# Leaves of the block factorisation: half of T's rows turned by TensorE during the leaf, and one PSUM area per stage

## Chip, cores and metric

One core of a Trainium2 chip. The metric is the device time of one launch in microseconds (us); the median of three runs of the kernel before is 1134.49 us (1133.51 to 1136.28).

## The reference, cut to what matters

The layer is x + FFN/2, then x + attention, then x + FFN/2 (widths 256 and 1024, ternary weights, 8 sequences of 1024 tokens). The change lies in the attention, which is a recurrence over tokens with a 128 x 128 state:

```python
u = k / (norm(k) + EPS)
Au = A @ u;  denom = 1 + u @ Au
A = A - outer(Au, Au) / denom
z = Au / denom
M = M + outer(v, (k @ q) * z)
o = M @ q
```

The kernel computes it in chunks of 128 tokens: 8 chunks of 8 sequences are 64 "pairs", each with a 128 x 128 Gram matrix, and each such matrix is factorised as T K T' = D, with T lower triangular (unit diagonal) and D diagonal. This is done twice: once named "inv" (for the full inverse T) and once named "ldl" (applied to a right side, whose rows replace it).

## The kernel before

Five parts run one after the other: `feed_forward_keys`, `factorise(..., "inv", ...)` (from 332 us of the profiled execution to about 532), `gram`, `factorise(..., "ldl", ...)` (592 to about 795), and `outputs_feed_forward`. Each part is one block: every engine ends it before the next begins.

`factorise` works on all 64 pairs at once. The matrix is cut into NW = 4 block rows of W = 32 columns, and stage r (0 to 3) of a factorisation has a serial part and a wide part.

- The serial part is the **leaf**, on VectorE. `take(r)` (line 999) transposes the 64 diagonal blocks from PSUM so that one lane (partition) holds half a block's rows; `leaf(r)` (L1007 to L1033) runs 32 elimination steps of four instructions (shuffle a row L1011, reciprocal L1014, product L1026, update L1029), each waiting on semaphore `chain` for the one before. It fills `R`, whose columns W to 2W are the rows of the block's T. Then `turn(r)` (L1035) transposes all 32 rows of T, 32 x 32 elements at a time, into `Tt` (L1039, 1024 elements a partition) and the pivots into `dT` (L1040), and raises `turned`. Of the 32 lanes of each quarter in `Tt`, 16 are read later (one for each pair).
- What follows on the way to the next leaf is `finish_diagonal(r + 1)` on TensorE (L1241): it waits for `turned`, multiplies by `Tt` (L1248, 64 products, each two matmuls and two weight loads in the records, so 128 of each), then VectorE (`over_d`, L1052) and ScalarE (`next_block`, L1097) read the result half and half, and a second set of 64 products (L1255) completes the next diagonal block, which `take(r + 1)` reads.
- The wide part runs on TensorE and ScalarE **while VectorE is in the leaf**. TensorE goes through the fills of stage r in program order (`done` L1168, `done right`, `panel` L1203, `panel right`, then `diagonal(r + 1)` L1228), each 4 PSUM banks in size, and ScalarE copies each to SBUF (`empty`, L1099; for `done` with 16 scaled copies more, L1123) and raises `emptied`. In "inv" TensorE also makes the queries and values (`qv`, L1260; 16 in all, 5, 4, 2 and 5 of them in the four stages) and the dot products (`dots`, L1277).
- The fills rotate over the areas in `works` (L789): one area of 4 banks in "inv", which has three other PSUM tiles, and **two areas** in "ldl". `free` (L871) makes a fill wait until the fill before it in the same area has been emptied, or the diagonal in it has been taken. So in "ldl" TensorE may fill one area while ScalarE empties the other.

Both engines take their queues in order. SyncE stores pivots (`keep_d`) and finished rows (`keep_rows`) behind the same semaphores.

Of the kernel before, what the change touches and what calls it, by code (L numbers as in the profile page):

```python
# [12 lines left out]
P = 128  # L13
# [17 lines left out]
W = 32  # L31
RW = W // 2
NW = P // W
NQ = NP // 4


def wait(eng, sem, value):
# [717 lines left out]
def factorise(nc, name, m, c, a=None):  # L755

    first = a is not None  # L760
    with ExitStack() as ctx:
        def sb(what, shape, dt=F32):
# [2 lines left out]
        def psum(what, shape, dt=F32):  # L765
            return ctx.enter_context(nc.psum_tensor(f"{name}_{what}", shape, dt))
# [5 lines left out]
        R = c.R  # L772
# [13 lines left out]
            ZR = sb("right_side", [P, NQ, P])  # L786
            YR = [m.T[:, NQ * k:NQ * (k + 1)] for k in range(NW)]

        works = [psum(f"work{i}", [P, NQ, P]) for i in range(1 if first else 2)]  # L789
        if first:  # L790
            wqv = sb("wqv", [P, DC, 2, H])
            bq = sb("bq_column", [P, 1])
# [10 lines left out]
        lane_reset = sem("lane_reset")  # L803
        chain = sem("lane_chain")
        turned = sem("turned")
        taken = sem("diagonal_taken")
        filled = sem("filled")
        emptied = sem("emptied")
# [6 lines left out]
        if first:  # L815
            w_in = sem("wqv_in")
            a_in = [sem(f"aT_in{s}") for s in range(2)]
            u_in = sem("uT_in")
            q_made = sem("q_product")
            q_done = sem("q_done")  # L820
            v_made = sem("v_product")
            v_done = sem("v_done")
            uq_done = sem("uq_done")
            dots_done = sem("dots_done")
            dots_kept = sem("dots_kept")
            q_stored = sem("q_stored")
            v_stored = [sem(f"v_stored{s}") for s in range(2)]

        def block_of(r):
            return slice(W * r, W * r + W)  # L830
# [63 lines left out]
        with nc.Block() as block:  # L894
# [95 lines left out]
            @block.vector  # L990
            def _(v):
                links = [0]

                def note(ins):
                    links[0] += 1
                    ins.then_inc(chain, 1)
                    return links[0]

                def take(r):

                    v.wait_ge(diag_done, r + 1)
                    nc.vector.transpose(M[:, :, 0:W].rearrange("l r (h p) -> l r h p", h=2),
                                        area(r, "diagonal")[:, :, 0:W].rearrange("i p (r h) -> i r h p", h=2)).then_inc(taken, 1)
                    v.wait_ge(taken, r + 1)
                    v.wait_ge(lane_reset, r + 1)

                def leaf(r):  # L1007
                    for j in range(W):
                        own = j % 2
                        v.wait_ge(chain, links[0])  # L1010
                        row = note(nc.vector.stream_shuffle(R[:, j, j:W + j + 1], M[:, j // 2, j:W + j + 1],  # L1011
                                                            [16 * own + i % 16 for i in range(W)]))
                        v.wait_ge(chain, row)
                        i = nc.vector.reciprocal(dl[:, j:j + 1], R[:, j, j:j + 1])  # L1014
                        if j == W - 1:
                            note(i)
                            break
                        note(i)

                        r0 = (j + 1) // 2
                        n = RW - r0
                        window = slice(j + 1, W + j + 1)
                        shape = [P, n, W]
                        note(nc.vector.tensor_tensor(prod[:, :n], M[:, r0:, j:j + 1].to_broadcast(shape),  # L1026
                                                     R[:, j:j + 1, window].to_broadcast(shape), ALU.mult))
                        v.wait_ge(chain, links[0])
                        i = nc.vector.scalar_tensor_tensor(out=M[:, r0:, window], in0=prod[:, :n],  # L1029
                                                           scalar=dl[:, j:j + 1], in1=M[:, r0:, window],  # L1030
                                                           op0=ALU.mult, op1=ALU.subtract, reverse1=True)
                        note(i)
                    v.wait_ge(chain, links[0])  # L1033

                def turn(r):  # L1035
                    if r:

                        v.wait_ge(filled, fill_number[r, "done" if first else "done right"] + 1)
                    nc.vector.transpose(Tt[:], R[:, :, W:])  # L1039
                    nc.vector.transpose(dT[r][:], dl[:]).then_inc(turned, 1)  # L1040

                def over_d(r):


                    v.wait_ge(turned, r + 1)
                    for half in range(2):
                        pr = slice(8 * half, 8 * half + 8)
                        if half:
                            v.wait_ge(y_done, 2 * r + 1)
                        else:  # L1050
                            v.wait_ge(next_done, r + 1)
                        nc.vector.scalar_tensor_tensor(  # L1052
                            out=YD[r][:, pr, 0:W], in0=area(r + 1, "diagonal")[:, pr, W:2 * W], scalar=-1.0,
                            in1=dT[r][:, pr].unsqueeze(2).to_broadcast([P, 8, W]),
                            op0=ALU.mult, op1=ALU.mult).then_inc(yd_done, 1)

                def times_q(r, which):

                    v.wait_ge(u_in, 16 * (QV_OF[r][-1] + 1))
                    for n in which:  # L1060
                        v.wait_ge(q_done, n + 1)
                        nc.vector.tensor_tensor(uT[:, slot(n)], uT[:, slot(n)], qT[:, slot(n)], ALU.mult
                                                ).then_inc(uq_done, 1)

                for r in range(NW):
                    take(r)
                    leaf(r)
                    turn(r)
                    if r < NW - 1:
                        if first:  # L1070
                            times_q(r, QV_OF[r][:3])
                        over_d(r)
                        if first:
                            times_q(r, QV_OF[r][3:])
                    elif first:
                        times_q(r, QV_OF[r])

            @block.scalar
            def _(act):
# [3 lines left out]
                def reset(r):  # L1083
                    if r:
                        act.wait_ge(turned, r)
                    copy(M[:, :, W:], c.lane_ident[:]).then_inc(lane_reset, 1)

                def next_block(r):

# [60 lines left out]
                for r in range(NW + 1):  # L1150
                    if 0 < r < NW - 1:
                        act.wait_ge(turned, r)
                        nc.scalar.mul(nd[:], dT[r - 1][:, 0:NQ], -1.0).then_inc(nd_done, 1)
                        act.wait_ge(nd_done, r)
                    for i, (what, n) in enumerate(beside(r)):
                        if what is not None:
                            empty(r, what)
                        if first and r and i == 0:
                            keep_dots(r - 1)
                        if n is not None:  # L1160
                            qv(n)
                    if r < NW - 1:
                        reset(r + 1)
                        next_block(r)

            @block.tensor
            def _(pe):
# [60 lines left out]
                def diagonal(r):  # L1228
# [9 lines left out]
                    if r == 0:  # L1238
                        i.then_inc(diag_done, 1)

                def finish_diagonal(r):  # L1241

                    k = r - 1
                    work = area(r, "diagonal")
                    emptied_of(pe, k, "panel")
                    pe.wait_ge(turned, r)
                    for p, q in tile_order():
                        i = nc.tensor.matmul(work[rows_of(q), p, W:2 * W], Tt[rows_of(q), :, p],  # L1248
# [39 lines left out]
                diagonal(0)  # L1288
                for r in range(NW + 1):
                    if r == NW:  # L1290
                        pe.wait_ge(turned, NW)
                    if first and 0 < r < NW:
                        dots(r - 1)
                    if first and r == 0:
                        pe.wait_ge(w_in, 48)
                    opened = r >= NW - 1
                    for what, n in beside(r):
                        if what is not None:
                            (done if what.startswith("done") else panel)(r, what)
                        elif not opened:  # L1300
                            diagonal(r + 1)
                            opened = True
                        if n is not None:
                            qv(n)
                    if not opened:
                        diagonal(r + 1)
                    if first and r == NW:
                        dots(r - 1)
                    if r < NW - 1:
                        finish_diagonal(r + 1)  # L1310

# [586 lines left out]
```

## Time and profile before

| | us |
|---|---|
| median of 3 runs | 1134.49 |
| the profiled execution's own time | 1137.41 |
| its span | 1135.7 |
| busy: TensorE, VectorE, ScalarE | 937.7, 806.5, 527.1 |
| "inv": start of its first diagonal to its last T transpose's end | 332.0 to 521.7 |
| "ldl": the same | 592.9 to 782.3 |

A timeline row gives start, length, engine, line, operation, the output and inputs, the number of instructions merged in it, and in brackets the idle time of the engine before it and what ended that; "issue" there means that the profile shows nothing that it waited for. Matmul rows merge many overlapping instructions.

### The profile page before, as it was taken

The page shows a single profiled execution, that of the slowest core. Times are in us where ns is not written, and L with a number is a line of the kernel's source. Part 1 is how long each engine was busy: PE and PEld are TensorE (multiplying, and loading weights), DVE is VectorE, ACT ScalarE, POOL GpSimd, SP SyncE. Part 2 cuts the span into 40 slices and gives each one's busy share as a digit, 9 for nine tenths or more (in the row PEclk, how much of TensorE's full clock was granted, in tenths as well). Part 3 has the DMA queues.
Part 4 walks back from the last instruction along what each step waited for, and adds up shares of the span by engine and source line. Part 5 has one row for each costly group of instructions (what it writes and reads, how often), then busy time and mean ns, then how long its engine had stood idle before and what let it go on. Part 6 is the DMA issues. An engine that isn't in the chain of part 4 may idle for free. (4 is left out here: it accounts for less than half of the span.)

```text
span 1135.7 us, 28433 instructions
## 1 busy us (share of the span) xinstructions
PE 937.7 (83%) x11466; PEld 724.9 (64%) x11466; DVE 806.5 (71%) x2564; ACT 527.1 (46%) x1083; POOL 300.6 (26%) x254
## 2 busy tenths in 40 slices
PE   4799999999967788686991445692689999999998
PEld 1477777777845667675980434581567777777766
DVE  6877778787659888794559797885366666666663
ACT  4677878777632142121331212101165655656564
POOL 4345344453210000000000000000475464645440
PEclk9999999999988697798996576796699999999999
DMA  5354554644258252154540000056344242434231
GB/s 150 66 131 107 135 130 121 161 110 130 94 173 206 87 159 74 44 156 126 149 129 1 3 2 5 3 151 136 117 102 103 66 121 75 102 94 99 61 75 56
DMA packets 185518, 113.92 MB, mean 100 GB/s; under 512 B 85808, under 2 KB 178352, under 8 KB 184752
## 3 DMA queue, kind: packets, MB, share of 16 engines
q1 hardware_dynamic: 168496, 95.38, 32.9%
q10 hardware_dynamic: 16896, 16.78, 4.8%
q8 instruction: 88, 1.44, 0.5%
q14 instruction: 38, 0.31, 0.1%
HBM read 49.16 MB, written 37.75 MB: 77 GB/s over the span
## 5 line engine op out<-in xcount | busy, mean ns | idle before, releaser
L1664 DVE TENSOR_TENSOR out_h_rest<-out_ps_h,out_h_high 128x512 f16<-128x512 f32 x128 | 88.4, 690 | 100.1 <-ACT out_ps_h L1726 99.4
L1574 POOL TENSOR_TENSOR T<-T,out_bv_rows 128x512 f32<-128x512 f32 x16 | 20.3, 1271 | 478.3 <-DMA out_bv_rows<-in_bqkv 477.3
L1725 ACT ACTIVATE out_h_high<-out_ps_h,b_columns 128x512 f16<-128x512 f32 x128 | 88.1, 689 | 110.8 <-PE out_ps_h L1807 109.7
L410 DVE TENSOR_TENSOR ffn_h_rest<-ffn_ps_h,ffn_h_high 128x512 f16<-128x512 f32 x128 | 87.0, 684 | 53.8 <-ACT ffn_ps_h L580 53.3
L1819 PE MATMUL out_ps_y<-w_ternary,out_h_high 128*128 128x256 f16 x512 | 118.2, 273 | 0.3 <-DVE out_h_rest L1664 0.3
L1819 PE MATMUL out_ps_y<-w_ternary,out_h_rest 128*128 128x256 f16 x512 | 118.2, 273 | 0.0
L579 ACT ACTIVATE ffn_h_high<-ffn_ps_h,b_columns 128x512 f16<-128x512 f32 x128 | 87.8, 686 | 65.0 <-PE ffn_ps_h L653 64.4
L667 PE MATMUL ffn_ps_y<-w_ternary,ffn_h_rest 128*128 128x256 f16 x512 | 117.8, 273 | 0.0
L667 PE MATMUL ffn_ps_y<-w_ternary,ffn_h_high 128*128 128x256 f16 x512 | 117.8, 273 | 0.0
L653 PE MATMUL ffn_ps_h<-ffn_xT_high,w_ternary 128*128 128x512 f16 x256 | 98.7, 386 | 11.7 <-DVE ffn_h_rest L410 11.7
L653 PE MATMUL ffn_ps_h<-ffn_xT_rest,w_ternary 128*128 128x512 f16 x256 | 98.4, 384 | 0.0
L1807 PE MATMUL out_ps_h<-out_xT_high,w_ternary 128*128 128x512 f16 x256 | 97.0, 379 | 0.0
L1807 PE MATMUL out_ps_h<-out_xT_rest,w_ternary 128*128 128x512 f16 x256 | 97.0, 379 | 0.0
L1726 ACT ACTIVATE out_ps_h<-out_ps_h,b_columns 128x512 f32<-128x512 f32 x128 | 84.0, 657 | 0.0
L580 ACT ACTIVATE ffn_ps_h<-ffn_ps_h,b_columns 128x512 f32<-128x512 f32 x128 | 83.9, 655 | 0.0
L1029 DVE SCALAR_TENSOR_TENSOR ldl_lane_matrix<-ldl_rank_one,ldl_lane_dinv,ldl_lane_matrix 128x480 f32<-128x480 f32 (+15 forms) x124 | 61.3, 494 | 4.4
L1029 DVE SCALAR_TENSOR_TENSOR inv_lane_matrix<-inv_rank_one,inv_lane_dinv,inv_lane_matrix 128x480 f32<-128x480 f32 (+15 forms) x124 | 61.3, 494 | 4.4
L1819 PEld LDWEIGHTS out_ps_y<-w_ternary,out_h_high 128*128 128x128 f16 x512 | 50.1, 98 | 17.5 <-DVE out_h_rest L1664 0.6
L667 PEld LDWEIGHTS ffn_ps_y<-w_ternary,ffn_h_rest 128*128 128x128 f16 x512 | 50.1, 98 | 17.0
L1819 PEld LDWEIGHTS out_ps_y<-w_ternary,out_h_rest 128*128 128x128 f16 x512 | 50.1, 98 | 17.0
L667 PEld LDWEIGHTS ffn_ps_y<-w_ternary,ffn_h_high 128*128 128x128 f16 x512 | 50.1, 98 | 16.9
L1248 PE MATMUL ldl_work<-ldl_panel,ldl_T_turned 32*32 32x32 f32 x384 | 6.1, 239 | 63.8 <-DVE ldl_dinv_turned L1040 63.8
(190 smaller groups left out, 2192.1 us busy)
## 6 DMA issues: line engine op xcount, KB each, us to landing
ffn_x<-in_x SPq DMA_DIRECT2D x16, 512.0 KB, 4.8
x_scratch<-ffn_x_out ACTq DMA_DIRECT2D x16, 512.0 KB, 3.3
aT_scratch<-ffn_aT SPq DMA_DIRECT2D x16, 512.0 KB, 5.4
inv_aT<-aT_scratch SPq DMA_DIRECT2D x16, 512.0 KB, 4.7
T<-x_scratch SPq DMA_DIRECT2D x16, 512.0 KB, 3.8
out_x<-out_x ACTq DMA_DIRECT2D x10, 512.0 KB, 3.3
uT_scratch<-ffn_uT SPq DMA_DIRECT2D x16, 256.0 KB, 5.4
inv_uT<-uT_scratch SPq DMA_DIRECT2D x16, 256.0 KB, 4.3
```

The costliest lines, as they stand in the source:

```text
L410: nc.vector.tensor_tensor(hl[n % 2][:, f], ps_h[f % 3][:], hh[n % 2][:, f], ALU.subtract).then_inc(hl_done, 1)
L579: nc.scalar.activation(hh[n % 2][:, f], ps_h[f % 3][:], ACT.Gelu, bias=c.b1[:, f:f + 1])
L580: nc.scalar.activation(ps_h[f % 3][:], ps_h[f % 3][:], ACT.Gelu, bias=c.b1[:, f:f + 1]).then_inc(g_done, 1)
L653: ins = nc.tensor.matmul(ps_h[f % 3][:], c.w1[:, d, f * P:(f + 1) * P], part[s][:, :, d], start=(k == 0), stop=(k == 2 * DC - 1))
L667: ins = nc.tensor.matmul(ps_y[t % 2][:], part[n % 2][:, f, t * P:(t + 1) * P], c.w2[:, f], start=(f == 0 and part is hh), stop=(f == FC - ...
L1029: i = nc.vector.scalar_tensor_tensor(out=M[:, r0:, window], in0=prod[:, :n], scalar=dl[:, j:j + 1], in1=M[:, r0:, window], op0=ALU.mult, o ...
L1574: nc.gpsimd.tensor_tensor(v0[s], v0[s], bv[:].unsqueeze(1).to_broadcast(group), ALU.add).then_inc(biased, 1)
L1664: nc.vector.tensor_tensor(hl[k % 2][:, f], ps_h[f % 3][:], hh[k % 2][:, f], ALU.subtract).then_inc(hl_done, 1)
L1725: nc.scalar.activation(hh[k % 2][:, f], ps_h[f % 3][:], ACT.Gelu, bias=c.b1[:, f:f + 1])
L1726: nc.scalar.activation(ps_h[f % 3][:], ps_h[f % 3][:], ACT.Gelu, bias=c.b1[:, f:f + 1]).then_inc(g_done, 1)
L1807: ins = nc.tensor.matmul(ps_h[f % 3][:], c.w1[:, d, f * P:(f + 1) * P], part[s][:, :, d], start=(j == 0), stop=(j == 2 * DC - 1))
L1819: ins = nc.tensor.matmul(ps_y[t % 2][:], part[k % 2][:, f, t * P:(t + 1) * P], c.w2[:, f], start=(f == 0 and part is hh), stop=(f == FC - ...
```

## The change

A constant EARLY = 16 is added. TensorE gets `turn_early(r)`: once row 15 of the leaf has been shuffled into `R`, 64 products of 128 x 32 elements of `R` with 16 columns of the unit matrix put the first 16 rows of T, turned, into a new PSUM tile `ps_t` (1 KB a partition, so one bank). It stands after all fills of stage r and after `diagonal(r + 1)`, ahead of `finish_diagonal(r + 1)`. ScalarE gets `early_rows(r)`, one copy of 256 elements a partition from `ps_t` to `Tt`, after all its emptying of stage r. VectorE's transpose at the leaf's end covers the other 16 rows. `finish_diagonal` and the last `done` wait for the copy too. `works` has one area in both factorisations.

```diff
+EARLY = W // 2
...
-        works = [psum(f"work{i}", [P, NQ, P]) for i in range(1 if first else 2)]
+        works = [psum("work", [P, NQ, P])]
+        ps_t = psum("ps_t", [P, EARLY, NQ])
...
+        CHAIN = 4 * W - 2
...
                         v.wait_ge(filled, fill_number[r, "done" if first else "done right"] + 1)
-                    nc.vector.transpose(Tt[:], R[:, :, W:])
+                    nc.vector.transpose(Tt[:, EARLY:], R[:, EARLY:, W:])
                     nc.vector.transpose(dT[r][:], dl[:]).then_inc(turned, 1)
...
+                def early_rows(r):
+                    act.wait_ge(early_made, r + 1)
+                    if r:
+
+                        act.wait_ge(filled, fill_number[r, "done" if first else "done right"] + 1)
+                    copy(Tt[:, :EARLY, 0:NQ], ps_t[:]).then_inc(early_done, 1)
...
+                    if r < NW:
+                        early_rows(r)
                     if r < NW - 1:
                         reset(r + 1)
                         next_block(r)
...
+                def turn_early(r):
+
+                    pe.wait_ge(chain, r * CHAIN + 4 * EARLY - 3)
+                    wait(pe, early_done, r)
+                    for j in range(EARLY):
+                        for q in range(4):
+                            i = nc.tensor.matmul(ps_t[rows_of(q), j, :], R[:, j, W:], c.ident[:, W * q:W * q + NQ],
+                                                 start=True, stop=True)
+                    i.then_inc(early_made, 1)
+
                 def finish_diagonal(r):
...
                     emptied_of(pe, k, "panel")
+                    pe.wait_ge(early_done, r)
                     pe.wait_ge(turned, r)
...
                     if r == NW:
+                        pe.wait_ge(early_done, NW)
                         pe.wait_ge(turned, NW)
...
                         dots(r - 1)
+                    if r < NW:
+                        turn_early(r)
                     if r < NW - 1:
                         finish_diagonal(r + 1)
```

## Rows read from the trace of the kernel before

**Rows 1.** Page of the profile: busy time by engine, and the queue that brings instructions.

```profile
PE 937.7 (83%) x11466; PEld 724.9 (64%) x11466; DVE 806.5 (71%) x2564; ACT 527.1 (46%) x1083; POOL 300.6 (26%) x254
...
q8 instruction: 88, 1.44, 0.5%
```

**Rows 2.** Lines L1039, L1040, L1002: ns min/median/max, starts; L1040: who waited (us, times).

```profile
L1039 DVE STREAM_TRANSPOSE inv_T_turned<-lane_rows x4: 1245/1245/1246, 374.3 to 520.5; 128x1024 f32<-128x1024 f32 x4
...
L1040 DVE STREAM_TRANSPOSE ldl_dinv_turned<-ldl_lane_dinv x4: 169/170/170, 636.4 to 782.3; 128x32 f32<-128x32 f32 x4
...
  PE ldl_work L1248: 63.8, 3
...
  PE inv_work L1248: 9.4, 2
...
L1002 DVE STREAM_TRANSPOSE inv_lane_matrix<-inv_work x4: 716/716/716, 333.1 to 479.3; 128x512 f32<-128x512 f32 x4
```

**Rows 3.** Timeline of VectorE: the sixteenth shuffle of the first ldl leaf.

```profile
618.13 0.19 DVE L1011 STREAM_SHUFFLE lane_rows<-ldl_lane_matrix 128x33 f32<-128x33 f32 x1
```

**Rows 4.** Timeline of TensorE, inv: the first products after each leaf, and the queue before.

```profile
375.81 2.04 PE L1248 MATMUL inv_work<-inv_panel,inv_T_turned 32*32 32x32 f32 x128 [6.28 <-DVE inv_dinv_turned L1040]
...
423.65 2.02 PE L1248 MATMUL inv_work<-inv_panel,inv_T_turned 32*32 32x32 f32 x128 [3.15 <-DVE inv_dinv_turned L1040]
...
470.60 0.80 PE L1235 MATMUL inv_work<-inv_panel_done,inv_panel_over_d 32*32 32x32 f32 x36 [3.26 <-issue]
471.51 1.57 PE L1248 MATMUL inv_work<-inv_panel,inv_T_turned 32*32 32x32 f32 x92
475.09 0.78 PE L1248 MATMUL inv_work<-inv_panel,inv_T_turned 32*32 32x32 f32 x36 [2.01 <-issue]
476.94 2.18 PE L1255 MATMUL inv_work<-inv_panel_done,inv_panel_over_d 32*32 32x32 f32 x128 [1.07 <-ACT inv_panel_done L1081]
...
521.88 5.10 PE L1177 MATMUL inv_work<-inv_panel,inv_T_turned 32*32 32x128 f32 x128 [2.92 <-DVE inv_dinv_turned L1040]
```

**Rows 5.** Timeline, inv: nearest operations to the added products and the added copy.

```profile
380.79 8.69 PE L1284 MATMUL inv_ps_dots<-causal,inv_uT 128*128 128x1 f32 x40
...
410.39 1.08 PE L1184 MATMUL inv_work<-KK,ident 128*32 128x128 f32 x32
...
475.95 0.38 ACT L1081 ACTIVATE inv_panel_done<-inv_work 128x256 f32<-128x256 f32 x1 [3.93 <-PE inv_work L1248]
```

**Rows 6.** Timeline of TensorE, ldl stage 2: pauses, and the wait at the leaf's end.

```profile
693.76 1.70 PE L1177 MATMUL ldl_work<-ldl_panel,ldl_T_turned 32*32 32x32 f32 x105 [1.64 <-issue]
...
697.12 3.98 PE L1177 MATMUL ldl_work<-ldl_right_side,ldl_T_turned 32*32 32x128 f32 x105 [0.37 <-issue]
...
704.60 1.56 PE L1197 MATMUL ldl_work<-ldl_panel_done,ldl_panel_over_d 32*32 32x32 f32 x128 [1.15 <-issue]
708.35 0.33 PE L1197 MATMUL ldl_work<-ldl_panel_done,ldl_panel_over_d 32*32 32x32 f32 x10 [2.18 <-issue]
...
726.09 1.35 PE L1235 MATMUL ldl_work<-ldl_panel_done,ldl_panel_over_d 32*32 32x32 f32 x75 [1.67 <-issue]
734.58 2.04 PE L1248 MATMUL ldl_work<-ldl_panel,ldl_T_turned 32*32 32x32 f32 x128 [7.14 <-DVE ldl_dinv_turned L1040]
```

**Rows 7.** Timeline of ScalarE, ldl stage 2: the emptying of the four fills.

```profile
696.26 2.98 ACT L1123 ACTIVATE ldl_panel_over_d<-ldl_work,ldl_minus_dinv 128x32 f32<-128x32 f32 x16
701.19 2.06 ACT L1081 ACTIVATE T<-ldl_work 128x512 f32<-128x512 f32 x4 [1.96 <-PE ldl_work L1177]
708.73 0.79 ACT L1081 ACTIVATE ldl_panel<-ldl_work 128x128 f32<-128x128 f32 x4 [5.48 <-PE ldl_work L1197]
721.45 2.06 ACT L1081 ACTIVATE ldl_right_side<-ldl_work 128x512 f32<-128x512 f32 x4 [11.93 <-PE ldl_work L1197]
```

**Rows 8.** Timeline of TensorE, ldl: the waits at the ends of leaves 1 and 3.

```profile
686.24 2.05 PE L1248 MATMUL ldl_work<-ldl_panel,ldl_T_turned 32*32 32x32 f32 x128 [20.83 <-DVE ldl_dinv_turned L1040]
...
782.48 6.19 PE L1177 MATMUL ldl_work<-ldl_right_side,ldl_T_turned 32*32 32x128 f32 x128 [15.95 <-DVE ldl_dinv_turned L1040]
```

More of the change, by code:

```diff
@@ L805, in factorise @@
         turned = sem("turned")
+        early_made = sem("early_rows_turned")
+        early_done = sem("early_rows_done")
         taken = sem("diagonal_taken")
```

## The prediction

> **What bounds the kernel now.** The page comes first: TensorE has the largest busy share, VectorE the next [rows 1], but a share of the whole span says nothing about the two factorisations, where the change lies. So I went to the source lines of the leaf's end. Who waits for the transposed pivots is the question there: in ldl TensorE waits 63.8 us in three stages, in inv only 9.4 us and only twice in three [rows 2]. The leaf is thus the bound in ldl, and in inv it barely is. The timeline of TensorE at each leaf's end gives its spare time one by one: 6.28, 3.15, nothing and 2.92 us in inv stages 0 to 3 [rows 4]; in ldl stages 1, 2 and 3 20.83, 7.14 and 15.95 us [rows 6, 8], and so 63.8 - 20.8 - 7.1 = 35.9 us in stage 0. In inv stage 2 the first product at L1248 starts at 471.51 behind the last of L1235 without a wait: TensorE itself is the bound there. Last, the pauses "issue", in which TensorE waits for nothing shown: they end 128 matmuls apart (36 + 92 between 470.60 and 475.09; 128 and 10 at 704.60 and 708.35) [rows 4, 6]. 2 x 11466 matmuls and weight loads over 88 packets on the instruction queue is 261 a packet [rows 1], so one packet is about 128 pairs. I read the pauses as waits for instructions: from the end of one pause to the end of the next it takes 4.49, 3.36 and 3.75 us, while 128 short pairs last 2.0 us.
>
> **Removed.** VectorE's transpose of T takes 1245 ns for 1024 elements, the one of 32 takes 169 [rows 2]. Linearly, 512 elements are 169 + 480 x 1.085 = 690 ns; the bounds are half (622) and the 512 elements from PSUM (716). I take 0.54 us saved a leaf, 4.3 us over eight, where the leaf is what TensorE waits for.
>
> **Added: 64 products.** They appear as 128 pairs. Nothing in the trace has this shape. The low bound is L1248 with as many pairs and 32-column weights, 2.04 us, or 15.9 ns each [rows 4]. The high bound is the dot products, 8.69 us / 40 = 217 ns with 128-column weights [rows 5]; a quarter of the columns is 54 ns, 6.95 us in all, below which the 34 ns of L1184 lie (weights of just this shape, but 128 columns streamed). I take 2.0 us if instructions are there, since columns loaded and streamed are no more than at L1248, and 3.7 us if TensorE comes from a burst, by the pauses' spacing. Then ScalarE's copy of 256 elements, 0.38 us [rows 5], plus 0.2 us for two handovers: 0.6 us. The wait for the sixteenth shuffle binds nowhere: in the first ldl leaf that is over at 618.3, some 17 us before the leaf ends [rows 3].
>
> On the Trainium skill: its page "Runtime: NRT & Kernel Launch", section "Instruction fetch mechanics", says that a block of 256 instructions is fetched while the one before runs and that this is mostly hidden. The block's size agrees with 261 a packet; the pauses speak against the hiding. By that rule the added products would cost 2.0 us everywhere; that case is a rival below.
>
> **Inv, stage by stage.** Stage 0: 2.0 + 0.6 fits in 6.28: -0.5 us. Stage 1: 2.6 us against 3.15 - 0.54 = 2.6: the start is no later than the new leaf's end, but three blocks of 128 pairs now follow each other where there were two. Before, these took from 420.5 (423.65 less the idle 3.15) to about 428.7, 8.2 us; after, two to three supply times, 7.4 to 11.1 us, so -0.5 to +2.9; I take +0.5. Stage 2 has no spare time, so the saving is lost and the addition is paid whole: 3.7 + 0.6, of which some 0.4 overlaps the arrival of the next block: +3.9 us. Stage 3: 2.6 against 2.92 - 0.54: -0.2 us. Inv together +3.7 us.
>
> **Ldl: the second area goes.** Stages 0, 1 and 3 have 35.9, 20.83 and 15.95 us spare; what follows adds at most some 17 us to one of them (stage 1, with longer copies), so I take -0.5 each, -1.6 in all. Stage 2 is the one to work out, 7.14 us spare [rows 6]. With one area every fill waits for ScalarE to empty the one before. `done` must wait for the diagonal to be taken, 0.72 us [rows 2], which hides in the pause of 1.64 us. `done right` started at 695.46 and will wait for the scaled copies, which end at 699.24: +3.9. `panel` waits for 2.06 us of copies, `panel right` for 0.79, `diagonal(3)` for 2.06 [rows 7]; each with 0.2 us of handover: +2.3, +1.0, +2.3. Sum 9.5 us. The waits give the instruction supply time: of the four later pauses, 0.37 + 1.15 + 2.18 + 1.67 = 5.4 us, I take 2.5 away (the two that come right behind a wait, and a bit). After idling, a product of 128 columns runs at the rate of 6.19 us for 128 instead of 3.98 for 105 [rows 6, 8]: +0.9. The early products follow the burst of L1235: 3.7 + 0.6 = 4.3. That makes 9.5 - 2.5 + 0.9 + 4.3 = 12.2 us against 7.14, 5.1 us late, and nothing of the 0.54 is gained. L1248 and L1255 then run behind a burst, as in inv stage 2, where a pause of 2.01 us fell into them [rows 4]: +1.3. Stage 2 gives +6.4.
>
> **Sum.** +3.7 - 1.6 + 6.4 = +8.5 us. Against the profiled execution's 1137.41 that is 1145.9; the median of the runs is 2.9 us lower, so 1143.0. Elsewhere nothing changes: the other parts start after a barrier, and SyncE's stores of `W` start some 5 us later behind the fill of stage 3 but have 16 us before the last one.
>
> **Rivals.**
> *Instructions are not what it waits for.* If the pauses have another cause, and stay as they are, the added products cost 2.0 us: inv -0.5 - 0.5 + 2.6 - 0.2, ldl stage 2 12.2 - 1.7 - 7.1 = 3.4, the others -1.6: +3.2 us, 1137.7. The spacing of 128 pairs speaks against it. Chance 0.13.
> *Lost overlap is cheap.* If the waits for ScalarE swallow all later pauses, ldl stage 2 is 9.5 - 5.4 + 4.3 - 7.1 = +1.3: in all +3.4, 1137.9. For it: the sum of pauses is large; against it: two of them lie within one burst of 256 pairs. Chance 0.09.
> *The weight loads are exposed.* At 54 ns a pair the addition is 6.95 + 0.6 = 7.55 us: inv 1.3 + 4.4 + 7.55 + 4.6, ldl stage 2 12.2 - 4.3 + 7.55 - 7.1 = 8.3, the others -1.6: +24.6, 1159.1. L1184's 34 ns with all its streaming speak against it; anything between is possible. The Trainium skill's "TensorEngine Tiling (Array Packing)", "Instruction Overhead", has about 60 cycles of overhead for each matmul, so an estimate by that page is 128 x 25 ns = 3.2 us at 2.4 GHz; the 15.9 ns of L1248 show it overlapped. Chance 0.11.
> *Faster.* TensorE and ScalarE do it all in time and each leaf gives its 0.54 us: -4.3 us, 1130.2. The place is TensorE's spare time at the leaf's end; it decides once that is above 2.6 us in all eight stages. Seven stages might have it if pauses vanish, inv stage 2 has none now, and would need its pause of 3.26 us [rows 4] gone. Chance 0.05.
>
> **How the numbers follow.** The forecast (instruction supply and lost overlap as above) has 0.62, with its own range 1139 to 1149. About 0.3% (3.4 us) is what a measurement of this kernel can tell from no change. The two rivals near +3.3 us lie on that bound: of their 0.22 I give 0.13 to no change and 0.09 to slower. Slower 0.62 + 0.11 + 0.09 = 0.82, same 0.13, faster 0.05. For 8 in 10 the range takes in the two rivals at 1137.7 and 1137.9 and goes up to a price of some 30 ns a pair: 1136 to 1152.
>
> **What would show it.** L1039 at about 0.69 us, eight times. In inv stage 2 L1248 starting some 4 to 5 us later after the leaf's last transpose, with the copy to `Tt` as what ended the wait. In ldl stage 2 TensorE idle before each fill with ScalarE as releaser, and the leaf's end no longer what L1248 waits for. The added products at about 2 us in ldl stages 0 and 3 and near 3.7 in stage 2. Wrong if L1248 in ldl stage 2 still waits for `dinv_turned`, if the pauses do not come every 128 pairs, or if the products take over 4 us where TensorE was idle before.

## The result, and the profile after

The changed kernel takes 1149.79 us, median of 4 runs (1147.88 to 1153.38), against 1134.72 for the kernel before: ratio 1.0129, 95% interval 1.0113 to 1.0146, 15 us slower. The forecast was 1143.0 us with a range of 1136 to 1152 and 0.82 on slower.

First the two prices. The source lines of the changed kernel (ns min/median/max, first and last start):

```profile
L1047 DVE STREAM_TRANSPOSE inv_T_turned<-lane_rows x4: 711/712/712, 375.1 to 530.2; 128x512 f32<-128x512 f32 x4
```

```profile
L1264 PEld LDWEIGHTS inv_ps_t<-ident,lane_rows x512: 106/109/157, 368.5 to 531.2; 128*32 128x32 f32 x171
L1264 PE MATMUL inv_ps_t<-ident,lane_rows x512: 182/183/236, 368.5 to 531.2; 128*32 128x16 f32 x171
```

The transpose fell from 1.245 [rows 2] to 0.712 us, 0.53 us in each of the eight leaves. Where do 15 us come from? I cut the span at VectorE's transposes: a **leaf** runs from the start of `take` (L1002; L1010 in the changed kernel) to the end of the pivots' transpose (L1040; L1048), and a **stretch** from there to the next `take`. Each number is the difference of two such rows:

| stretch, us | inv 0 | inv 1 | inv 2 | ldl 0 | ldl 1 | ldl 2 |
|---|---|---|---|---|---|---|
| before | 5.29 | 5.31 | 7.92 | 7.03 | 5.81 | 5.46 |
| changed | 5.52 | 10.80 | 12.73 | 8.62 | 5.73 | 14.10 |
| difference | +0.2 | +5.5 | +4.8 | +1.6 | -0.1 | +8.6 |

The leaves went from 42.55 to 42.04 us, 0.51 us each. The six stretches cost 20.7 us and the eight leaves give 4.1 back; from the last leaf of inv to the first product of `gram` it is 14.86 instead of 15.40 us. That makes +16.0; the two profiled spans differ by 12.4, and the remaining -3.6 us lie in parts that the change does not touch (0.7 more ahead of the first `take`, 2.1 less in `gram`, 2.3 less in the output part). The medians of the kernel before in the comparisons below lie between 1135.7 and 1136.7 us, single runs between 1132 and 1141, so a few us of one execution are chance. A single stretch varies too: the one after inv stage 2, with TensorE's instructions of before, has 7.9 us in the kernel before, and 8.2 and 10.4 in two kernels below that change only ldl.

The timeline of TensorE in the changed kernel, inv stages 1, 2 and 3 (start, length, operation, count, idle time before it and its cause):

```profile
421.30 1.27 PE L1264 MATMUL inv_ps_t<-ident,lane_rows 128*32 128x16 f32 x128
423.60 1.68 PE L1276 MATMUL inv_work<-inv_panel,inv_T_turned 32*32 32x32 f32 x103 [1.03 <-DVE inv_dinv_turned L1048]
428.61 0.57 PE L1276 MATMUL inv_work<-inv_panel,inv_T_turned 32*32 32x32 f32 x25 [3.33 <-issue]
430.29 1.61 PE L1283 MATMUL inv_work<-inv_panel_done,inv_panel_over_d 32*32 32x32 f32 x103 [1.11 <-ACT inv_panel_done L1089]
433.64 0.58 PE L1283 MATMUL inv_work<-inv_panel_done,inv_panel_over_d 32*32 32x32 f32 x25 [1.74 <-issue]
...
476.60 0.56 PE L1252 MATMUL inv_work<-inv_panel_done,inv_panel_over_d 32*32 32x32 f32 x36 [2.97 <-issue]
477.08 1.17 PE L1264 MATMUL inv_ps_t<-ident,lane_rows 128*32 128x16 f32 x91
480.27 0.73 PE L1264 MATMUL inv_ps_t<-ident,lane_rows 128*32 128x16 f32 x37 [2.02 <-issue]
481.53 1.54 PE L1276 MATMUL inv_work<-inv_panel,inv_T_turned 32*32 32x32 f32 x91 [0.53 <-issue]
484.84 0.78 PE L1276 MATMUL inv_work<-inv_panel,inv_T_turned 32*32 32x32 f32 x37 [1.77 <-issue]
486.69 2.18 PE L1283 MATMUL inv_work<-inv_panel_done,inv_panel_over_d 32*32 32x32 f32 x128 [1.07 <-ACT inv_panel_done L1089]
...
530.16 1.27 PE L1264 MATMUL inv_ps_t<-ident,lane_rows 128*32 128x16 f32 x128
531.92 3.72 PE L1194 MATMUL inv_work<-inv_panel,inv_T_turned 32*32 32x128 f32 x128 [0.49 <-ACT inv_T_turned L1089]
```

Stage 1: the early products take 1.27 us and are done before the leaf ends. What is lost comes after the leaf: two pauses "issue", 3.33 and 1.74 us, exactly 128 matmuls apart (25 + 103). In the kernel before L1248 has no pause there [rows 4], nor has L1255. Stage 2: TensorE was the bound already; the 1.9 us of products hold a pause of 2.02 us, and the next pause stands again 128 matmuls on (37 + 91). Stage 3: the copy ends last.

That a pause is a wait for instructions is seen in the DMA view of the 3.3 us from 425.3 to 428.6: the queue that brings instructions starts one packet in it.

```profile
q8 instruction: 1, 0.02, 1.8%
```

One packet in one window proves little, but its time does: it starts at 426.36, 2.25 us before the pause ends. The same holds for the other pauses "issue" of 0.6 us and more in the changed kernel's rows of this section: each ends 2.2 to 2.7 us after a packet of this queue has started. In the shorter pauses the start lies ahead of the pause: the two of ldl stage 0 below hold no packet, theirs start at 643.70 and 648.52.

The timeline of TensorE in ldl, stages 0 and 2:

```profile
624.98 1.91 PE L1264 MATMUL ldl_ps_t<-ident,lane_rows 128*32 128x16 f32 x128 [12.16 <-DVE lane_rows L1019]
...
642.76 2.04 PE L1276 MATMUL ldl_work<-ldl_panel,ldl_T_turned 32*32 32x32 f32 x122 [15.87 <-DVE ldl_dinv_turned L1048]
646.05 0.33 PE L1276 MATMUL ldl_work<-ldl_panel,ldl_T_turned 32*32 32x32 f32 x6 [1.25 <-issue]
647.42 1.93 PE L1283 MATMUL ldl_work<-ldl_panel_done,ldl_panel_over_d 32*32 32x32 f32 x122 [1.04 <-ACT ldl_panel_done L1089]
650.86 0.33 PE L1283 MATMUL ldl_work<-ldl_panel_done,ldl_panel_over_d 32*32 32x32 f32 x6 [1.50 <-issue]
...
706.32 5.47 PE L1194 MATMUL ldl_work<-ldl_right_side,ldl_T_turned 32*32 32x128 f32 x128 [3.83 <-ACT ldl_panel_over_d L1138]
713.99 1.08 PE L1201 MATMUL ldl_work<-KK,ident 128*32 128x128 f32 x32 [2.21 <-ACT T L1089]
...
722.35 5.95 PE L1201 MATMUL ldl_work<-W,ident 128*32 128x512 f32 x32 [0.91 <-ACT ldl_panel L1089]
...
737.93 1.08 PE L1201 MATMUL ldl_work<-KK,ident 128*32 128x128 f32 x32 [2.17 <-ACT ldl_right_side L1089]
...
743.63 0.62 PE L1264 MATMUL ldl_ps_t<-ident,lane_rows 128*32 128x16 f32 x50
746.56 1.26 PE L1264 MATMUL ldl_ps_t<-ident,lane_rows 128*32 128x16 f32 x78 [2.31 <-issue]
748.36 0.97 PE L1276 MATMUL ldl_work<-ldl_panel,ldl_T_turned 32*32 32x32 f32 x49 [0.54 <-issue]
749.92 1.36 PE L1276 MATMUL ldl_work<-ldl_panel,ldl_T_turned 32*32 32x32 f32 x79 [0.60 <-issue]
```

In inv stage 2 and here the 0.53 and 0.54 us ahead of L1276, called "issue", are the time of ScalarE's copy. In ldl stage 0 TensorE had been idle for 15.87 us and still pauses after 122 and again 128 matmuls later: the idle time does not bring the next block, for no packet of the queue starts between 612.85 and 643.70. In ldl stage 2 it waits four times for ScalarE's emptying, 3.83 + 2.21 + 0.91 + 2.17 = 9.1 us, ends the last fill at 743.6, after the leaf (741.05), and only then turns the early rows.

### The profile page after: what moved, and what is told of

Same layout as the page of the kernel before. It is cut to its first block and busy times, and to the rows that moved or that the text cites. A ratio compares the mean times of both kernels' runs of the same rounds, so it can differ in the third digit from the quotient of the medians.

```text
span 1148.1 us, 30502 instructions
## 1 busy us (share of the span) xinstructions
PE 958.2 (83%) x12490; PEld 739.3 (64%) x12490; DVE 802.9 (70%) x2564; ACT 530.5 (46%) x1091; POOL 301.3 (26%) x254
## 5 line engine op out<-in xcount | busy, mean ns | idle before, releaser
L654 PE MATMUL ffn_ps_h<-ffn_xT_high,w_ternary 128*128 128x512 f16 x256 | 98.9, 386 | 11.1 <-DVE ffn_h_rest L411 11.0
L1629 POOL TENSOR_TENSOR out_xn_rest<-out_xn,out_xn_high 128x1024 f16<-128x1024 f32 x16 | 34.1, 2129 | 72.7 <-ACT out_xn_high L1750 72.7
```

The source lines that it names most:

```text
L654: ins = nc.tensor.matmul(ps_h[f % 3][:], c.w1[:, d, f * P:(f + 1) * P], part[s][:, :, d], start=(k == 0), stop=(k == 2 * DC - 1))
L1629: nc.gpsimd.tensor_tensor(xl[:], xn[:], xh[:], ALU.subtract).then_inc(xl_done, 1)
```

## The experiments

Two things changed at once, so the first four take them apart and try a cure for each. The stretches of all runs stand in one table at the end of this section; each is read from one execution. "us slower" is the measured ratio put on the median of the kernel before; the plain medians can differ from it by some 2 us (5.3 instead of 7.4 us with products only).

**One area, nothing else.** The kernel before with

```diff
-        works = [psum(f"work{i}", [P, NQ, P]) for i in range(1 if first else 2)]
+        works = [psum(f"work{i}", [P, NQ, P]) for i in range(1)]
```

> The kernel before with one PSUM area in ldl and nothing else of the change. What is read is the stretch from the end of the transposed pivots to the next diagonal's transpose (before: 5.29, 5.31, 7.92 us in inv, 7.03, 5.81, 5.46 in ldl). If the lost area alone delays TensorE past the leaf's end in ldl stage 2: the last of these rises from 5.5 to 8 to 9 us and the kernel is 2 to 4 us slower, the others as before. Rival, the area costs nothing without the added products (7.14 us of spare time cover it): the stretch stays at 5.5 us and the time within 0.1%.

Measured: ratio 1.0057 (1.0039 to 1.0074), 6.5 us slower; ldl stage 2 10.94 us. The area costs by itself, and more than expected. Not all of it is that stage: ldl stage 0, which was to stay as before, rose from 7.03 to 8.84 us. TensorE at the end of ldl stage 2 in this run (the leaf ended at 739.00):

```profile
741.08 1.06 PE L1235 MATMUL ldl_work<-ldl_panel_done,ldl_panel_over_d 32*32 32x32 f32 x76 [2.08 <-issue]
741.96 1.01 PE L1248 MATMUL ldl_work<-ldl_panel,ldl_T_turned 32*32 32x32 f32 x52
744.74 1.36 PE L1248 MATMUL ldl_work<-ldl_panel,ldl_T_turned 32*32 32x32 f32 x76 [1.77 <-issue]
```

The last fill ends 3 us after the leaf, and the products behind the leaf then run in the same burst as `diagonal(3)` and meet its pauses.

**The change in inv alone.** `EARLY_IN` is the tuple of stages with early rows; ldl has none, and two areas.

```diff
+        EARLY_IN = (0, 1, 2, 3) if first else ()
...
-                    nc.vector.transpose(Tt[:, EARLY:], R[:, EARLY:, W:])
+                    own = EARLY if r in EARLY_IN else 0
+                    nc.vector.transpose(Tt[:, own:], R[:, own:, W:])
```

> The change in inv alone; ldl keeps its two areas and the whole transpose. If the changed kernel's profile reads right (inv stretches 5.5, 10.8 and 12.7 us, leaves 0.53 us shorter): 8 us slower than before, ldl unchanged. Rival, the prediction's sum for inv: +3.7 us, with 10.8 a chance of that one execution (then nearer 6.5).

Measured: 1.0039 (1.0021 to 1.0058), 4.4 us slower and not the 8 expected; the rival was nearer. Stage 2 has 13.81 us as in the changed kernel, stage 1 only 7.78, with the same instructions of TensorE:

```profile
423.73 1.70 PE L1282 MATMUL inv_work<-inv_panel,inv_T_turned 32*32 32x32 f32 x103 [3.42 <-DVE inv_dinv_turned L1054]
425.72 0.57 PE L1282 MATMUL inv_work<-inv_panel,inv_T_turned 32*32 32x32 f32 x25 [0.29 <-issue]
```

The pauses stand after the same 103 matmuls, but the first lasts 0.29 us and not 3.33. So its place is given by the code and its length by when the packet comes. When that is can be read from four kernels with these products in inv stage 1:

| us | products start, ahead of the leaf's end | packet starts, behind the products' start | behind the leaf's end | first pause |
|---|---|---|---|---|
| changed | 2.16 | 5.06 | 2.90 | 3.33 |
| full, two areas | 2.04 | 4.54 | 2.50 | 3.06 |
| inv alone | 4.55 | 4.50 | -0.05 | 0.29 |
| products only, inv | 4.24 | 4.30 | 0.06 | 0.54 |

The packet comes 4.3 to 5.1 us after the products begin in all four. What differs most is how far ahead of the leaf's end TensorE gets to them. Ldl stage 0, whose code is that of before, has 5.35 us instead of 7.03.

**The change in full, two areas kept.** The early rows go into the first bank of the area that is free at that point:

```diff
+        def turned_area(r):
+            if first:
+                return ps_own[:]
+            other = area(r + 1, fills_of(r + 1)[0])
+            return other[:, 0:EARLY * NQ // P].rearrange("p a (b c) -> p (a b) c", c=NQ)
```

> The change in full, but ldl keeps two areas: the early rows go into the first bank of the area that is free at that point. If the lost area is what makes ldl stage 2 late: its stretch falls from 14.1 to 5.5 to 7.5 us, and the kernel is 7 to 9 us above before, all from inv. Rival, the added products behind the burst do it by themselves: the stretch stays above 10 us and the kernel is 12 us or more above before.

Measured: 1.0041 (1.0026 to 1.0056), 4.7 us slower, less than the 7 to 9 expected. Ldl stage 2 falls from 14.10 to 5.64 us. TensorE there, in this run:

```profile
734.31 0.88 PE L1275 MATMUL ldl_work<-ident,lane_rows 128*32 128x16 f32 x49
736.69 1.27 PE L1275 MATMUL ldl_work<-ident,lane_rows 128*32 128x16 f32 x79 [1.50 <-issue]
741.17 2.06 PE L1287 MATMUL ldl_work<-ldl_panel,ldl_T_turned 32*32 32x32 f32 x128 [3.22 <-DVE ldl_dinv_turned L1056]
```

The early products are over 3.1 us before the leaf's end (741.03), so the lost area, and not the products, is what made this stage late. By the differences of the ratios, the second area's loss holds 0.88 of the change's 1.29% with the products behind it, and 0.57 alone, each with some 0.2 of uncertainty and with what moved in ldl stage 0.

**Early products ahead of the last query and value product (inv), two areas.**

```diff
                         if n is not None:
+                            if n == QV_OF[r][-1] and r in EARLY_IN:
+                                turn_early(r)
                             qv(n)
```

> As the run with two areas, and in inv the early products (and their copy) stand ahead of the stage's last query and value product instead of behind it. Same number of instructions, same rows. If pauses for instructions come from where the products stand (a burst right ahead of the leaf's end): the stretch after inv stage 1 falls from 10.8 to 5.3 to 6.5 us, the one after stage 2 from 12.7 to 8 to 11, and the kernel is 1 to 5 us above before. Rival, the number of instructions alone counts: both stay, 7 to 9 us above before.

Measured: 1.0018 (0.9998 to 1.0038), inv stages 1 and 2 9.43 and 10.27 us. Stage 2 as expected; stage 1 is not, since its products now meet the pause themselves and hold the last `qv` up. The place helps stage 2 (14.03 in the run before this one), but TensorE remains the bound in both. For the whole kernel the intervals of the two runs overlap, and the profiled execution lies 5 us above this kernel's median.

**Products only.** Inv with the added products and nothing that reads them: whole transposes, no copy, no wait for it. This leaves out the use of the early rows, not a part of the result.

```diff
-                    own = EARLY if r in EARLY_IN else 0
+                    own = 0
...
-                    if r in EARLY_IN:
-                        early_rows(r)
```

> Inv with the 64 added products in each stage, but nobody reads them: VectorE turns all rows, ScalarE copies nothing, TensorE does not wait for the copy; ldl as before. If the products as instructions are the cost: stretches after inv stages 1 and 2 are 7 to 10.5 and 11 to 13.5 us, the leaves are as long as before (42.55), the kernel 7 to 10 us slower than before. Rival, the handover over ScalarE is the cost: the stretches fall to 5.3 to 6 and 10 us, under 3 us slower.

Measured: 1.0065 (1.0045 to 1.0084), 7.4 us slower, stretches 8.30 and 12.57 us, leaves of 42.56. The instructions are the cost. The handover over ScalarE is at most a small part of it: stage 2 has 12.57 us without it, and 12.73, 13.81 and 14.03 in the three kernels with it, whose leaves are 0.5 us shorter.

**Does the place of a block matter?** Three kernels only move TensorE's instructions, by unused products ahead of each factorisation's first diagonal (n = 16 and 63 in the kernel before, 12 in the changed one):

```diff
+                for i in range(n):
+                    q = i % 4
+                    nc.tensor.matmul(works[0][rows_of(q), 0, 0:16], c.ident[:, block_of(q)], c.ident[:, 0:16],
+                                     start=True, stop=True)
                 diagonal(0)
```

> The kernel before with 16 unused products (32 pairs of weight load and matmul) put ahead of each factorisation's first diagonal, which only moves all later instructions of TensorE by 32 pairs. If a block of instructions is asked for at a place that moves with the code, and pauses depend on where that place lies to the waits: stretches change with no work added, above all the one after ldl stage 0, whose pause of 1.47 us sat after 124 pairs of L1255: it comes after 92 of L1248 or 60 to 92 of L1255 and is under 1 us, the stretch 5.4 to 6.5 us instead of 7.0; inv stages 1 and 2 within 1.5 us of 5.3 and 7.9. Rival, pauses are given by the amount of work alone: all six stretches within 0.3 us of before.

Measured: 1.0014 (0.9999 to 1.0029). Ldl stage 0 falls from 7.03 to 5.64 us as expected; what was not expected is stage 1, 9.32 instead of 5.81:

```profile
683.18 1.92 PE L1248 MATMUL ldl_work<-ldl_panel,ldl_T_turned 32*32 32x32 f32 x120 [18.84 <-DVE ldl_dinv_turned L1040]
687.16 0.34 PE L1248 MATMUL ldl_work<-ldl_panel,ldl_T_turned 32*32 32x32 f32 x8 [2.05 <-issue]
688.54 1.82 PE L1255 MATMUL ldl_work<-ldl_panel_done,ldl_panel_over_d 32*32 32x32 f32 x120 [1.04 <-ACT ldl_panel_done L1081]
691.96 0.33 PE L1255 MATMUL ldl_work<-ldl_panel_done,ldl_panel_over_d 32*32 32x32 f32 x8 [1.60 <-issue]
```

This is the picture of ldl stage 0 of the changed kernel: a block's end 8 pairs ahead of the leaf's end here and 6 there, and pauses although TensorE had idled for 18.84 and 15.87 us. A stretch got 3.5 us longer with no work added to it.

> The same with 63 unused products (126 pairs, so the blocks lie 2 pairs later in inv and 4 in ldl; some 2 us longer at each start). By the place theory the stretch after inv stage 1, without a pause before, gets one of 1 to 2 us in L1255 (7 us instead of 5.3), since the next block is asked for only behind the wait ahead of L1255. Rival, amount alone: 5.3 us as before.

Measured: 1.0002 (0.9979 to 1.0024). A miss: inv stage 1 has 5.63 us and no pause. My rule for when the next block is asked for was too fine.

> The changed kernel with 12 unused products (24 pairs) ahead of each factorisation. By the place theory the pause in the products behind inv stage 1 (3.33 us after 103 pairs, then 1.74 after 103 more) comes 24 pairs sooner but the second block is asked for sooner: stretch 7 to 10 us instead of 10.8; ldl stage 0 loses its pause of 1.25 (8.6 becomes 7 or less). Rival, amount alone: 10.8 and 8.6 within 0.5 us.

Measured: 1.0156 (1.0122 to 1.0191), from two runs only. Half a miss: ldl stage 0 falls from 8.62 to 5.67 us, but inv stage 1 keeps 11.49, and ldl stage 1 rises from 5.73 to 8.69, with pauses after 126 matmuls.

**Where the change does pay.** Early rows in ldl alone, two areas (`EARLY_IN = () if first else (0, 1, 2, 3)`):

> The early rows in ldl alone, with two areas kept; inv is the kernel before. Ldl leaves 0.53 us shorter each. If only what the early products meet in inv and the lost area made the change slow: no slower than before, 2 us faster at most, since the stretch after ldl stage 0 has its two pauses (8.6 to 9.2 us, as with two areas) or, if the blocks lie better, 5.4. Rival, the added products cost by themselves in ldl too: 2 us or more slower.

Measured: 1.0003 (0.9988 to 1.0019). The leaves are 0.53 us shorter, but stage 0 has 9.18 us. Then the same with 50 unused products ahead of the early ones of ldl stage 0:

```diff
+                    for i in range(50 if r == 0 and not first else 0):
+                        q = i % 4
+                        nc.tensor.matmul(ps_t[rows_of(q), 0, :], c.ident[:, block_of(q)], c.ident[:, 0:NQ],
+                                         start=True, stop=True)
                     for j in range(EARLY):
```

> The same, with 50 unused products ahead of the early ones in ldl stage 0, where TensorE idles, so that the blocks of instructions after it lie 100 pairs elsewhere and none ends within 30 pairs ahead of a leaf's end in stages 0 to 2. Place theory: stretches 5.3 to 6.3 us all three, 3 to 4 us faster than before. Rival, amount alone: as without the move, or slower.

Measured: 0.9983 (0.9967 to 0.9998), 1.9 us faster where 3 to 4 were expected; the three stretches are as expected. Ldl stage 0 without and with the move:

```profile
636.85 2.05 PE L1292 MATMUL ldl_work<-ldl_panel,ldl_T_turned 32*32 32x32 f32 x124 [15.87 <-DVE ldl_dinv_turned L1061]
640.71 0.32 PE L1292 MATMUL ldl_work<-ldl_panel,ldl_T_turned 32*32 32x32 f32 x4 [1.82 <-issue]
642.07 1.93 PE L1299 MATMUL ldl_work<-ldl_panel_done,ldl_panel_over_d 32*32 32x32 f32 x123 [1.04 <-ACT ldl_panel_done L1102]
645.51 0.32 PE L1299 MATMUL ldl_work<-ldl_panel_done,ldl_panel_over_d 32*32 32x32 f32 x5 [1.50 <-issue]
```

```profile
635.26 2.05 PE L1296 MATMUL ldl_work<-ldl_panel,ldl_T_turned 32*32 32x32 f32 x128 [14.50 <-DVE ldl_dinv_turned L1061]
638.38 0.53 PE L1303 MATMUL ldl_work<-ldl_panel_done,ldl_panel_over_d 32*32 32x32 f32 x23 [1.07 <-ACT ldl_panel_done L1102]
639.44 1.61 PE L1303 MATMUL ldl_work<-ldl_panel_done,ldl_panel_over_d 32*32 32x32 f32 x105 [0.53 <-issue]
```

More work, and the stretch is 6.03 instead of 9.18 us. The two intervals of the whole kernel overlap; the stretches are clearer than they. The kernel before with the same 50 products in ldl stage 0 (written to the area that is free there):

> The kernel before with the same 50 unused products at the same place and nothing of the change. Place theory: the stretch after ldl stage 0 falls from 7.0 to 5.4 us, the others stay under 6.3, the kernel 1 to 2 us faster than before or unchanged within its uncertainty. Rival: 7.0, 5.8, 5.5 as before.

Measured: 0.9999 (0.9980 to 1.0018), ldl stretches 5.42, 5.64, 5.61: the pause of before in stage 0 goes, 1.6 us of that stretch, too little for the whole kernel's time to show. (The 10.35 us after inv stage 2 in its row of the table is no effect of the move, which comes later.) Last, early rows in inv stages 0 and 3 too, where TensorE has spare time:

> The early rows in ldl (two areas, blocks moved by 100 pairs) and in inv stages 0 and 3, ahead of the last query and value product there. Two more leaves are 0.53 us shorter: 4 to 5 us faster than before, if the moved blocks of inv bring no pause. Rival: the added instructions of stage 0 and 3 move inv's blocks and cost as much as they gain, no faster than without them.

Measured: 1132.00 us, 0.9973 (0.9956 to 0.9989). This one is faster than both kernels, 3.1 us below before by the ratio, where 4 to 5 were expected. That the early rows of inv add to it is not shown: its interval overlaps that of the run without them.

| stretch, us | ratio | inv 0 | inv 1 | inv 2 | ldl 0 | ldl 1 | ldl 2 |
|---|---|---|---|---|---|---|---|
| one area only | 1.0057 | 5.77 | 5.54 | 8.19 | 8.84 | 5.84 | 10.94 |
| inv alone | 1.0039 | 5.63 | 7.78 | 13.81 | 5.35 | 5.86 | 5.45 |
| full, two areas | 1.0041 | 5.55 | 10.52 | 14.03 | 9.16 | 6.10 | 5.64 |
| ahead of the last qv | 1.0018 | 5.64 | 9.43 | 10.27 | 6.91 | 6.27 | 6.05 |
| products only, inv | 1.0065 | 5.50 | 8.30 | 12.57 | 5.35 | 5.72 | 5.58 |
| before, moved by 16 | 1.0014 | 5.76 | 6.30 | 6.70 | 5.64 | 9.32 | 6.46 |
| before, moved by 63 | 1.0002 | 5.37 | 5.63 | 8.84 | 7.02 | 6.06 | 5.28 |
| changed, moved by 12 | 1.0156 | 6.52 | 11.49 | 10.97 | 5.67 | 8.69 | 15.13 |
| ldl alone | 1.0003 | 5.28 | 5.83 | 8.47 | 9.18 | 5.78 | 6.40 |
| ldl alone, moved by 50 | 0.9983 | 5.28 | 5.82 | 8.47 | 6.03 | 5.80 | 5.69 |
| before, ldl moved by 50 | 0.9999 | 5.28 | 5.54 | 10.35 | 5.42 | 5.64 | 5.61 |
| ldl moved, inv 0 and 3 | 0.9973 | 5.54 | 5.33 | 8.19 | 5.80 | 5.53 | 5.95 |

## Why the prediction was right, and where its terms were off

The sign, the mechanisms and the two places that carry most of the cost (inv stage 2, ldl stage 2) were as predicted; the sum was 8.5 us and the measured change 15. The measured time is 6.8 us above the forecast and 2.2 below the upper end of the range; that it lies inside owes something to the range's width, for two terms (inv stage 1, ldl stage 0) carry 6.1 us that the sum did not have. The signs that were named came: in inv stage 2 the first product behind the leaf starts 5.2 us after its end instead of 0.15, in ldl stage 2 it no longer waits for the leaf, and none of the three signs of being wrong is there. Term by term, each as stretch plus leaf of the profiled execution:

- **Removed**: 0.54 us a leaf predicted; 0.53 measured on the transpose, 0.51 on the leaf.
- **Price of the 128 pairs**: 2.0 us predicted, 1.27 measured in inv stage 1 and 1.91 at the first ldl leaf (granted clock 1.00 and 0.50 there, 2.4 and 1.2 GHz). Where a pause falls into them they took 3.9 us (inv stage 2) and 4.2 (ldl stage 2) for the 3.7 predicted. The rival of exposed weight loads is out; the row of L1248 was the right neighbour.
- **Inv stage 2**: +3.9 predicted, +4.3 measured (4.8 less 0.5). The lack of spare time and the supply of instructions did what was said, and the run with products only shows it without the handover.
- **Inv stage 1**: +0.5 predicted, +5.0 measured, the largest miss. The step that failed is "two to three supply times, 7.4 to 11.1 us" for three blocks: from 421.30 to 434.22 it took 12.9. I took the next block to be asked for early enough; it arrived 3.33 us late, then 1.74. The term is also unsteady: with the same instructions of TensorE another kernel lost only 2.5 us on the stretch, because TensorE got to the early products 4.55 and not 2.16 us ahead of the leaf's end.
- **Inv stage 3**: -0.2 predicted, -1.0 measured up to the start of `gram`. TensorE did start late, by 0.9 us instead of 0.05 after the leaf, but its product took 3.72 us instead of 5.10 [rows 4]. The granted clock was 1.00 in it and 0.71 in the kernel before, where TensorE had idled for 2.92 us ahead of it instead of 0.49. That gain was not forecast and is luck.
- **Ldl stage 0**: -0.5 predicted, +1.1 measured. "35.9 us spare" was taken to cover everything; spare time does not help against a boundary that lies just ahead of the wait. One area alone gives 8.84, two areas with early products 9.16, so the added work is not the cause. What differs is whether a block more came before the wait. In the kernel before packets start at 600.04 and then 640.75 (the leaf ends at 636.53); with one area alone at 593.90 and then 640.14 (leaf's end 639.17), so there the one before the wait is missing.
- **Ldl stage 2**: +6.4 predicted, +8.1 measured. The waits for ScalarE were 9.1 us against 9.5 predicted. Too small was what follows: the stretch holds 2.31 us of pause, 0.54 of copy and 0.60 of pause up to the end of L1276. And I had taken 2.5 of 5.4 us of pauses away as swallowed by the waits; three of the four stayed nearly whole (1.09, 1.93 and 1.70 us for 1.15, 2.18 and 1.67 [rows 6]). The run with one area alone had +5.5 us here, where the same sum without the early products, 12.2 - 4.3 - 7.1 + 1.3, gives 2.1.
- **The rest**: inv stage 0 -0.5 predicted, -0.3 measured; ldl stages 1 and 3 -1.0 predicted for the two, -0.6 and -0.5 measured.

The rival that instructions are not what it waits for is out: moving the code moves the pauses, the two of a pair are 127 or 128 matmuls apart in the rows shown here, and a packet of the instruction queue starts 2.2 to 2.7 us before the end of each of the changed kernel's. The Trainium skill, "Runtime: NRT & Kernel Launch", section "Instruction fetch mechanics", has the block's size right (256 instructions); its "mostly hidden" does not hold in this kernel, where pauses of 0.3 to 3.3 us stand between blocks of short matmuls.

What stays open: exactly where in a block the next one is asked for (one run on it missed, one half missed). In inv stage 1 the packet starts 4.3 to 5.1 us behind the early products' start; in stage 2 of the changed kernel it starts 1.5 us after the pause before it ends (476.60, 478.06). Loads of `aT` run in stage 1 in all four kernels; whether they delay the packet was not tried.

## What to carry to other kernels

Before moving work to an engine that "is idle during the leaf", read its spare time stage by stage at the point where the result is needed: here one stage in eight had none and one had less than the second area was worth. Count instructions as well as microseconds: 128 pairs of 10 to 16 ns cost some 3.7 us of supply when they join a burst (476.60 to 480.27). And when a small change makes a stage slower that it does not touch, look for pauses with no releaser at a fixed spacing before explaining it otherwise.

## What the runs showed that was not expected

A stretch between two leaves changed by up to 3.5 us with no work added to it, by where TensorE's blocks of 128 pairs lay: 5.35 to 7.03 us in ldl stage 0 with the work of before, 6.03 and 9.18 with early rows, 5.8 and 9.3 in stage 1. In all six stretches over 8 us there, counting back 128 pairs from the first pause puts a block's end 2 to 8 pairs ahead of the leaf's end, and TensorE pauses twice although it had idled before. The kernel before has the same place in ldl stage 0 and one pause, so the place in pairs is not all of it:

```profile
639.79 1.93 PE L1255 MATMUL ldl_work<-ldl_panel_done,ldl_panel_over_d 32*32 32x32 f32 x124 [1.07 <-ACT ldl_panel_done L1081]
643.20 0.32 PE L1255 MATMUL ldl_work<-ldl_panel_done,ldl_panel_over_d 32*32 32x32 f32 x4 [1.47 <-issue]
```

What differs there is one packet, which starts before the wait in this kernel and not in the one with one area alone. A hundred unused pairs at an idle place take the two pauses away and leave one of 0.53 us in that stretch.
